# Last attention: the causal mask of the scores with keys on partitions, as a bf16 identity product that begins their accumulation

## The chip, the cores and the metric

One Trainium2 chip, one core. The metric is the device time of one execution in microseconds (us). The kernel before took 2001.97 us, the median of three runs (2001.23 to 2002.74).

## The reference

A batch of 32 sequences of 128 tokens with 128 features goes through four gated blocks: an attention over a context (16 heads), a mixture of 64 small experts, a second attention over the context, and a block with a causal self-attention and 8 experts. The change touches the last block's self-attention alone. Cut to it:

```
h = _rmsnorm(x, g1)
c = h @ w_down                                   # 64 latent features
q = _rope(split(c @ wq), pos); k = _rope(split(c @ wk), pos); v = split(c @ wv)   # 16 heads of 4
scores = jnp.einsum('bhqd,bhkd->bhqk', q, k) / jnp.sqrt(jnp.float32(HD))
scores = jnp.where(causal, scores, -jnp.inf)
attn = jax.nn.softmax(scores, axis=-1)
o = jnp.einsum('bhqk,bhkd->bhqd', attn, v)
x = x + o @ w_up
```

## The kernel before

The program is written engine by engine with semaphores, in blocks that follow each other with a barrier between them. `attend_both_ways` (line 370) is called twice: for the first attention (names `a_att_...`, 120 keys, with limits on the scores, so `clamp` is true) and for the last one (names `dt_...`, 128 keys, `clamp` false, 1446 to 1674 us of the span). Only the second call is changed.

The function takes the 32 batches through a software pipeline of rounds t = 0 to 36. The 16 heads of a batch are four groups of four; a group's scores are one product of 512 columns that uses 32 rows of the array, and the groups use different rows. The scores are made twice. With queries on partitions they go into banks 0 and 1 (line 532), and VectorE takes the row maxima from there (`row_max`, line 658). With keys on partitions ("turned", line 538) they go into banks 2 to 5, one bank for each group, where the row maxima are subtracted by one more accumulating product (`shift`, line 546), ScalarE takes the exponential of two banks at a time (line 607), and the result is, without a transposition, the stationary operand of the product with the values (line 599). Scores are in two parts (high and low) in a reduced fp32 format, so each group needs three products.

In round t TensorE's own order is: phase one (`score_phase` with groups 0, 1 of batch t and turned groups 2, 3 of batch t-2), shift A of turned groups 0, 1 of batch t-2, the transpositions of lines 567 and 573, phase two (groups 2, 3 of batch t and turned groups 0, 1 of batch t-1), shift B of turned groups 2, 3 of batch t-2, lines 589 and 592, and the 32 small products of line 599. Ahead of phase one it waits for the first phase's buffers: the keys (`s_kd`), the second row maximum of batch t-1 (`s_max`) and exponential B (`s_expB`). Ahead of phase two it waits for this round's first row maximum (`s_max`), the queries (`s_qd`) and exponential A (`s_expA`).

The causal mask is a table of 0 and -1e30. For the scores with queries on partitions it is put in by TensorE: the two products of line 526, the identity in bf16 times the mask in bf16 (`causal16`), begin the accumulation in banks 0 and 1. For the turned scores VectorE adds the transposed mask in place, two banks of 512 columns at a time: `in_place`, line 667, called behind each row maximum; `s_inB` and `s_inA` count it, and TensorE waits for them ahead of shift B and shift A. In the first attention the same place holds the limits (line 665) instead of a mask.

The setup block at the program's start loads the tables; there GpSimd makes `ident16` and `causal16` (lines 210 and 211).

## Time and profile before

| what | value |
|---|---|
| median of three runs | 2001.97 us |
| the profiled execution's own time | 2003.22 us |
| its span, first to last instruction | 2001.4 us |
| granted clock of TensorE, mean over the span | 0.928 of full speed |
| TensorE products, busy | 1762.3 us (88%) |
| VectorE, busy | 1517.2 us (76%) |
| ScalarE, busy | 1146.6 us (57%) |
| GpSimd, busy | 1166.7 us (58%) |

PE is TensorE (PEld its weight loads, which overlap the products), DVE is VectorE, ACT ScalarE, POOL GpSimd, SP SyncE. The span is what lies between the first and the last instruction of the profiled execution; its own time is 1.8 us more, and 1.25 us above the median of the runs. Busy shares are means over stages with different limits, so a stage has to be read by itself. A timeline row gives start, busy time, engine, line and operation; "x2" behind it means that two instructions are merged, and the brackets give the idle time before it and what ended that.

### The profile page before, as it was taken

Reading aid. Unit: us, or ns where it says so; the run is one execution under the profiler, and the core shown is the slowest. Engines: PE = TensorE matmul, PEld = TensorE weight load, DVE = VectorE, ACT = ScalarE, POOL = GpSimd, SP = SyncE. Lnnn points to the kernel's source line nnn. Section 1 sums busy time; section 2 is a strip of 40 time slices with the busy share of each in tenths; the row PEclk is TensorE's granted clock in tenths of the full one; section 3 lists DMA queues with packets and bytes.
Section 4 is the critical chain, followed back from the end, with each engine's and each line's share of the span. In section 5 each row is a group of like instructions: output and inputs, shape, how many; then the busy total and the mean of one; then the engine's idle time right before and its main releaser. Section 6 shows DMA issues by size and latency. Waiting matters only on the chain. (4 is left out here: it accounts for less than half of the span.)

```text
span 2001.4 us, 37718 instructions
## 1 busy us (share of the span) xinstructions
PE 1762.3 (88%) x11570; PEld 1339.4 (67%) x11570; DVE 1517.2 (76%) x3061; ACT 1146.6 (57%) x2941; POOL 1166.7 (58%) x1158
## 2 busy tenths in 40 slices
PE   3688877799999999994899999996789997799998
PEld 2355555588888888872677777775535555588886
DVE  5699978677887787767666766675769997677876
ACT  1366645555555555552677777775436666455554
POOL 4777736567776777655233333323768884667764
PEclk9699977799999999995999999998869997799999
DMA  5111100555556566430000000000000000222222
GB/s 126 47 45 46 48 17 14 129 137 136 146 143 144 129 145 146 128 83 8 5 5 5 5 5 5 1 1 1 0 1 1 0 1 17 72 79 64 82 66 69
DMA packets 99645, 115.22 MB, mean 58 GB/s; under 512 B 18064, under 2 KB 55120, under 8 KB 99504
## 3 DMA queue, kind: packets, MB, share of 16 engines
q1 hardware_dynamic: 96576, 112.14, 21.7%
q10 hardware_dynamic: 2928, 1.39, 0.3%
q8 instruction: 66, 1.08, 0.2%
q14 instruction: 75, 0.61, 0.1%
HBM read 101.82 MB, written 3.28 MB: 53 GB/s over the span
## 5 line engine op out<-in xcount | busy, mean ns | idle before, releaser
L76 POOL TENSOR_TENSOR b_moe_hid_low<-b_moe_hid,b_moe_hid_high 128x512 fp32r<-128x512 f32 x256 | 331.3, 1294 | 173.2 <-ACT b_moe_hid_high L1038 171.5
L1044 ACT ACTIVATE bank<-bank 128x512 f32<-128x512 f32 x384 | 223.5, 582 | 339.8 <-PE bank L83 339.8
L1744 POOL TENSOR_TENSOR XC<-XC,c_recip 128x480 f32<-128x480 f32 x128 | 126.8, 991 | 292.6 <-DVE c_recip L1911 292.6
L1069 DVE TENSOR_TENSOR b_moe_gu<-bank,XC 128x512 f32<-128x512 f32 x256 | 176.6, 690 | 115.7 <-PE bank L83 100.0
L76 POOL TENSOR_TENSOR e_moe_hid_low<-e_moe_hid,e_moe_hid_high 128x512 fp32r<-128x512 f32 x128 | 165.6, 1294 | 84.2 <-ACT e_moe_hid_high L1038 83.4
L1865 ACT ACTIVATE XC<-bank,c_shift 128x120 f32<-128x120 f32 x512 | 176.9, 364 | 21.2 <-DVE c_shift L1901 21.2
L71 DVE CAST c_ts_high<-bank 128x480 fp32r<-128x480 f32 x128 | 84.2, 658 | 135.0 <-PE bank L83 134.3
L1074 DVE TENSOR_TENSOR b_moe_hid<-bank,b_moe_gu 128x512 f32<-128x512 f32 x256 | 176.9, 691 | 9.3 <-POOL b_moe_hid_low L76 0.7
L1038 ACT ACTIVATE b_moe_hid_high<-b_moe_hid 128x512 fp32r<-128x512 f32 x256 | 160.0, 625 | 12.4 <-DVE b_moe_hid L1074 11.6
L1860 ACT ACTIVATE c_probT<-bank 120x512 f32<-120x512 f32 x128 | 76.6, 598 | 105.1 <-PE bank L1790 103.2
L1069 DVE TENSOR_TENSOR e_moe_gu<-bank,XC 128x512 f32<-128x512 f32 x128 | 88.4, 690 | 62.2 <-PE bank L83 51.0
L1865 ACT ACTIVATION_READ_ACCUMULATOR XC<-bank,c_shift 128x1 f32 x512 | 108.7, 212 | 0.0
L607 ACT ACTIVATE dt_probT<-bank 128x1024 f32<-128x1024 f32 x64 | 65.5, 1024 | 69.9 <-PE bank L546 69.9
L81 PE MATMUL bank<-b_moe_hid_high,b_moe_wd_high 128*128 128x512 f32 x256 | 100.0, 391 | 1.6 <-POOL b_moe_hid_low L76 1.6
L658 DVE TENSOR_REDUCE dt_negmax<-bank 128x8 f32<-128x1024 f32 x64 | 78.4, 1224 | 30.0 <-PE bank L532 13.4
L81 PE MATMUL bank<-XT_high,b_moe_wg_high 128*128 128x512 f32 (+1 forms) x256 | 100.2, 391 | 0.9 <-PEq L1181 0.9
L81 PE MATMUL bank<-XT_high,b_moe_wu_high 128*128 128x512 f32 (+1 forms) x256 | 100.2, 392 | 0.8 <-DVE b_moe_gu L1069 0.8
L83 PE MATMUL bank<-XT_low,b_moe_wg_high 128*128 128x512 f32 (+1 forms) x256 | 100.1, 391 | 0.0
L82 PE MATMUL bank<-XT_high,b_moe_wg_low 128*128 128x512 f32 (+1 forms) x256 | 100.1, 391 | 0.0
L83 PE MATMUL bank<-XT_low,b_moe_wu_high 128*128 128x512 f32 (+1 forms) x256 | 99.9, 390 | 0.0
L82 PE MATMUL bank<-XT_high,b_moe_wu_low 128*128 128x512 f32 (+1 forms) x256 | 99.9, 390 | 0.0
L83 PE MATMUL bank<-b_moe_hid_low,b_moe_wd_high 128*128 128x512 f32 x256 | 99.6, 389 | 0.0
(386 smaller groups left out, 5622.9 us busy)
## 6 DMA issues: line engine op xcount, KB each, us to landing
XC<-b_comb SPq DMA_DIRECT2D x256, 256.0 KB, 4.4
XC<-e_comb SPq DMA_DIRECT2D x64, 256.0 KB, 3.1
X<-in_x SPq DMA_DIRECT2D x4, 512.0 KB, 9.0
a_att_qs_high<-XC SPq DMA_DIRECT2D x32, 64.0 KB, 1.8
a_att_qs_low<-a_Q_low SPq DMA_DIRECT2D x32, 64.0 KB, 1.9
a_att_ks_high<-a_K_high SPq DMA_DIRECT2D x32, 64.0 KB, 1.9
a_att_ks_low<-a_K_low SPq DMA_DIRECT2D x32, 64.0 KB, 1.9
b_moe_w_gate<-in_b_wgT SPq DMA_DIRECT2D x8, 256.0 KB, 3.0
```

What stands on the lines that cost most here:

```text
L71: return eng.tensor_copy(high.bitcast(F32R), x)
L76: return eng.tensor_tensor(low.bitcast(F32R), x, high, ALU.subtract)
L81: pe.matmul(out, w[0].bitcast(F32R), x[0].bitcast(F32R), start=start, stop=False)
L82: pe.matmul(out, w[1].bitcast(F32R), x[0].bitcast(F32R), start=False, stop=False)
L83: return pe.matmul(out, w[0].bitcast(F32R), x[1].bitcast(F32R), start=False, stop=stop)
L658: return dve.tensor_reduce(negmax[u][:].rearrange("p (b r h) -> p b r h", b=2, r=2)[:, half], banks[:, 0:2, 0:HG * nk].rearrange("p b (h k ...
L1038: act.activation(hid_high[k % 4][:].bitcast(F32R), hid[k % 2][:], ACT.Copy).then_inc(s_hh, 1)
L1044: act.activation(gate_b[j % 4][:], gate_b[j % 4][:], ACT.Silu).then_inc(s_silu, 1)
L1069: dve.tensor_tensor(gu[j % 2][:], up_b[j % 2][:], comb[j // 2][:, (j % 2) // share, :], ALU.mult).then_inc(s_gu, 1)
L1074: dve.tensor_tensor(hid[j % 2][:], gate_b[j % 4][:], gu[j % 2][:], ALU.mult).then_inc(s_p, 1)
L1744: pool.tensor_tensor(prob[r % 8], prob[r % 8], recip[:, r % 8, :].unsqueeze(2).broadcast_to([P, HG, NKV]), ALU.mult).then_inc(s_norm, 1)
L1865: e = act.activation(prob[n % 8][:, h, :], score_b[n % 2][:, h * NKV:(h + 1) * NKV], ACT.Exp, bias=shift[:, n % 8, h:h + 1], accum_out=sum ...
```

## The change

A second bf16 mask, `causalT16`, is made by GpSimd at the end of the setup block: the transposed mask four times side by side, 128x512. In the last attention `score_phase` now issues, behind the two products of line 526 and ahead of the scores, one identity product per turned group (two in each phase, line 532 of the changed kernel) that begins the accumulation in that group's bank; the first turned score product accumulates onto it instead of starting. VectorE's in-place addition is gone there, with the counts `s_inA` and `s_inB` and TensorE's two waits for them. The first attention keeps its in-place limits and its waits. The values in the table are the same, 0 and -1e30 rounded to bf16.

```diff
@@ -141,6 +141,7 @@
         causal = sb("causal", [P, P])
         causalT = sb("causalT", [P, P])
         causal16 = sb("causal16", [P, HG, P], BF16)
+        causalT16 = sb("causalT16", [P, HG, P], BF16)
         ident16 = sb("ident16", [P, P], BF16)
 
         prep = ExitStack()
@@ -209,6 +210,7 @@
                 pool.wait_ge(s_load, all_loads)
                 pool.tensor_copy(ident16[:], ident[:])
                 pool.tensor_copy(causal16[:], causal[:].unsqueeze(1).broadcast_to([P, HG, P]))
+                pool.tensor_copy(causalT16[:], causalT[:].unsqueeze(1).broadcast_to([P, HG, P]))
 
             @staticmethod
             def vector(dve):
@@ -525,6 +527,10 @@
                             for g in groups:
                                 pe.matmul(bank[g % 2][:], ident16[:], causal16[:].rearrange("p h k -> p (h k)"),
                                           start=True, stop=False)
+                        if not clamp and has(bt):
+                            for g in turned:
+                                pe.matmul(turned_b[g][:], ident16[:], causalT16[:].rearrange("p h q -> p (h q)"),
+                                          start=True, stop=False)
                         for qp, kp in ((0, 0), (0, 1), (1, 0)):
                             if has(t):
                                 for g in groups:
@@ -537,7 +543,7 @@
                                     rows = group_rows(g)
                                     i = pe.matmul(turned_b[g][:], ks[vt][kp][rows, :].bitcast(F32R),
                                                   qd[vt % 2][qp][rows].rearrange("p h q -> p (h q)").bitcast(F32R),
-                                                  start=(qp + kp == 0), stop=(qp == 1))
+                                                  start=(clamp and qp + kp == 0), stop=(qp == 1))
                         return i
 
                     def shift(u, groups):
@@ -558,7 +564,8 @@
                         if has(t) or has(t - 2):
                             score_phase(t, v, (0, 1), t - 2, (v - 2) % 4, (2, 3)).then_inc(s_first, 1)
                         if has(t - 2):
-                            pe.wait_ge(s_inA, t - 1)
+                            if clamp:
+                                pe.wait_ge(s_inA, t - 1)
                             pe.wait_ge(s_mrow, t - 1)
                             shift(u, (0, 1)).then_inc(s_shA, 1)
                         if has(t - 4):
@@ -579,7 +586,8 @@
                         if has(t) or has(t - 1):
                             score_phase(t, v, (2, 3), t - 1, (v - 1) % 4, (0, 1)).then_inc(s_second, 1)
                         if has(t - 2):
-                            pe.wait_ge(s_inB, t - 1)
+                            if clamp:
+                                pe.wait_ge(s_inB, t - 1)
                             shift(u, (2, 3)).then_inc(s_shB, 1)
                         if has(t - 1):
                             pe.wait_ge(s_mrow, t)
@@ -661,17 +669,14 @@
 
                     def in_place(half):
                         both = banks[0:nk, 2 + 2 * half:4 + 2 * half, :]
-                        if clamp:
-                            return dve.tensor_scalar(both, both, limit[0:nk, 0:1], limit[0:nk, 1:2], ALU.min, ALU.max)
-                        both = both.rearrange("p b (h q) -> p (b h) q", h=HG)
-                        return dve.tensor_tensor(both, both, causalT[:].unsqueeze(1).broadcast_to([P, 2 * HG, P]), ALU.add)
+                        return dve.tensor_scalar(both, both, limit[0:nk, 0:1], limit[0:nk, 1:2], ALU.min, ALU.max)
 
                     def body(t, v):
                         u = v % 2
                         if has(t):
                             dve.wait_ge(s_first, t + 1)
                             row_max(t, u, 0).then_inc(s_max, 1)
-                        if has(t - 2):
+                        if clamp and has(t - 2):
                             dve.wait_ge(s_first, t + 1)
                             in_place(1).then_inc(s_inB, 1)
                         if has(t - 4):
@@ -685,7 +690,7 @@
                         if has(t):
                             dve.wait_ge(s_second, t + 1)
                             row_max(t, u, 1).then_inc(s_max, 1)
-                        if has(t - 1):
+                        if clamp and has(t - 1):
                             dve.wait_ge(s_second, t + 1)
                             in_place(0).then_inc(s_inA, 1)
                         if has(t):
```

One phase two of a steady round on TensorE, from its mask products to the product of line 589, before (`ident` and `causal` stand for the bf16 copies; line numbers are those of each kernel):

```order
L526 MATMUL bank<-causal,ident 128x512 x2
L532 MATMUL bank<-dt_kd_high,dt_qs_high 128x512 x2
L538 MATMUL bank<-dt_qd_high,dt_ks_high 128x512 x2
L532 MATMUL bank<-dt_kd_low,dt_qs_high 128x512 x2
L538 MATMUL bank<-dt_qd_high,dt_ks_low 128x512 x2
L532 MATMUL bank<-dt_kd_high,dt_qs_low 128x512 x2
L538 MATMUL bank<-dt_qd_low,dt_ks_high 128x512 x2
L546 MATMUL bank<-dt_mrow,dt_ones_r 128x512 x2
L589 MATMUL bank<-w_d_up,dt_headT 128x128
```

and the same place of the changed kernel:

```order
L528 MATMUL bank<-causal,ident 128x512 x2
L532 MATMUL bank<-causalT,ident 128x512 x2
L538 MATMUL bank<-dt_kd_high,dt_qs_high 128x512 x2
L544 MATMUL bank<-dt_qd_high,dt_ks_high 128x512 x2
L538 MATMUL bank<-dt_kd_low,dt_qs_high 128x512 x2
L544 MATMUL bank<-dt_qd_high,dt_ks_low 128x512 x2
L538 MATMUL bank<-dt_kd_high,dt_qs_low 128x512 x2
L544 MATMUL bank<-dt_qd_low,dt_ks_high 128x512 x2
L552 MATMUL bank<-dt_mrow,dt_ones_r 128x512 x2
L597 MATMUL bank<-w_d_up,dt_headT 128x128
```

Two products of 128x512 are new, between the mask products that were there and the scores; the rest stands in the same order. It is so in both phases of every round in which there are turned scores.

On VectorE a round of the last attention, before:

```order
L658 TENSOR_REDUCE dt_negmax<-bank 128x8
L667 TENSOR_TENSOR bank<-bank,causalT 128x1024
L680 RECIPROCAL dt_recip<-bank 128x16
L683 TENSOR_TENSOR dt_heads<-bank,dt_recip 128x128
L658 TENSOR_REDUCE dt_negmax<-bank 128x8
L667 TENSOR_TENSOR bank<-bank,causalT 128x1024
L71 CAST dt_mz<-dt_negmax 128x4x4
L76 TENSOR_TENSOR dt_mz<-dt_negmax,dt_mz 128x4x4
L709 TENSOR_TENSOR XC<-bank,XC 128x128
```

and of the changed kernel:

```order
L666 TENSOR_REDUCE dt_negmax<-bank 128x8
L685 RECIPROCAL dt_recip<-bank 128x16
L688 TENSOR_TENSOR dt_heads<-bank,dt_recip 128x128
L666 TENSOR_REDUCE dt_negmax<-bank 128x8
L71 CAST dt_mz<-dt_negmax 128x4x4
L76 TENSOR_TENSOR dt_mz<-dt_negmax,dt_mz 128x4x4
L714 TENSOR_TENSOR XC<-bank,XC 128x128
```

The two in-place additions are gone and nothing takes their place.

## Rows read from the trace of the kernel before

**Rows 1.** The page, busy time of each engine over the whole span
```profile
PE 1762.3 (88%) x11570; PEld 1339.4 (67%) x11570; DVE 1517.2 (76%) x3061; ACT 1146.6 (57%) x2941; POOL 1166.7 (58%) x1158
```

**Rows 2.** Groups by line, 1450 to 1690 us (busy, mean ns; idle before, releasers)
```profile
L658 DVE TENSOR_REDUCE dt_negmax<-bank 128x8 f32<-128x1024 f32 x64 | 78.4, 1224 | 30.0 <-PE bank L532 13.4 <-PE bank L538 11.7
L667 DVE TENSOR_TENSOR bank<-bank,causalT 128x1024 f32<-128x1024 f32 x64 | 78.2, 1222 | 1.5 <-PE bank L538 1.5
...
L526 PE MATMUL bank<-causal,ident 128*128 128x512 bf16 x128 | 42.0, 412 | 29.5 <-ACT dt_probT L607 17.7 <-POOL dt_kd_low L489 6.7 <-DVE dt_negmax L658 5.1
```

**Rows 3.** Windows (length; busy of PE, PEld, DVE, ACT, POOL; PEclk): steady stretch, one round
```profile
1540.00:1570.00 30.00, 27.33 (x343) 15.93 (x340) 28.58 (x45) 20.29 (x49) 25.44 (x35) 1.00 0.00 0
1560.05:1566.28 6.23, 5.63 (x74) 3.31 (x72) 5.87 (x10) 4.21 (x10) 5.15 (x8) 1.00 0.00 0
```

**Rows 4.** Timeline of one round (start us, us, engine line op; idle before <-releaser)
```profile
1560.05 1.22 DVE L658 TENSOR_REDUCE dt_negmax<-bank 128x8 f32<-128x1024 f32 x1
...
1560.35 1.02 ACT L607 ACTIVATE dt_probT<-bank 128x1024 f32<-128x1024 f32 x1 [1.13 <-PE bank L546]
...
1561.19 1.22 DVE L667 TENSOR_TENSOR bank<-bank,causalT 128x1024 f32<-128x1024 f32 x1
...
1561.52 0.59 PE L526 MATMUL bank<-causal,ident 128*128 128x512 bf16 x2 [0.60 <-ACT dt_probT L607]
...
1562.62 0.39 PE L538 MATMUL bank<-dt_qd_low,dt_ks_high 32*128 32x512 f32 x1
...
1562.84 0.41 PE L546 MATMUL bank<-dt_mrow,dt_ones_r 32*128 32x512 f32 x2
1563.07 1.22 DVE L658 TENSOR_REDUCE dt_negmax<-bank 128x8 f32<-128x1024 f32 x1
...
1563.70 1.08 PE L599 MATMUL bank<-dt_probT,dt_vh 128*32 128x128 f32 x32
...
1564.21 1.22 DVE L667 TENSOR_TENSOR bank<-bank,causalT 128x1024 f32<-128x1024 f32 x1
...
1564.71 0.61 PE L526 MATMUL bank<-causal,ident 128*128 128x512 bf16 x2
...
1565.82 0.40 PE L538 MATMUL bank<-dt_qd_low,dt_ks_high 32*128 32x512 f32 x2
...
1566.06 0.40 PE L546 MATMUL bank<-dt_mrow,dt_ones_r 32*128 32x512 f32 x2
1566.28 1.23 DVE L658 TENSOR_REDUCE dt_negmax<-bank 128x8 f32<-128x1024 f32 x1
```

**Rows 5.** Line 546 over the whole kernel: what it waited for, us and times
```profile
  DVE bank L665: 31.4, 72
  DVE bank L667: 2.0, 3
```

**Rows 6.** Timeline of two phases in the stage's start, at the low clock
```profile
1467.06 1.01 PE L526 MATMUL bank<-causal,ident 128*128 128x512 bf16 x2 [1.43 <-DVE dt_negmax L658]
...
1471.29 1.01 PE L526 MATMUL bank<-causal,ident 128*128 128x512 bf16 x2 [0.81 <-ACT dt_probT L607]
```

**Rows 7.** Windows, columns as before, around the rise of the granted clock
```profile
1475.00:1480.00 5.00, 3.67 (x18) 1.62 (x19) 3.55 (x6) 2.19 (x7) 4.07 (x6) 0.50 0.00 0
1480.00:1485.00 5.00, 5.00 (x50) 2.69 (x48) 3.10 (x5) 2.36 (x7) 1.76 (x4) 0.50 0.00 0
1485.00:1490.00 5.00, 4.49 (x48) 2.44 (x50) 3.63 (x6) 2.75 (x7) 4.43 (x6) 0.97 0.02 3
```

**Rows 8.** Timeline near the stage's end
```profile
1664.28 0.50 PE L546 MATMUL bank<-dt_mrow,dt_ones_r 32*128 32x512 f32 x2 [0.74 <-DVE bank L667]
```

**Rows 9.** Timeline of the end of the setup block
```profile
34.70 0.61 POOL L211 CAST causal<-causal 128x512 bf16<-128x512 f32 x1
35.78 0.59 ACT L190 ACTIVATE mT<-bank 96x512 f32<-96x512 f32 x1 [1.11 <-PE bank L199]
```

**Rows 10.** Window, columns as before, of back-to-back 512-column products in the expert stage
```profile
1730.00:1750.00 20.00, 20.00 (x90) 16.48 (x89) 16.03 (x24) 11.65 (x21) 14.89 (x13) 1.00 0.30 97
```

## The prediction

> **What bounds the kernel now.** I read the page first: TensorE is busy for 88% of the span, VectorE for 76% [rows 1]. That is a mean over stages, so next the groups of the last attention, which alone is changed. There VectorE's two costliest groups are the row maxima and the mask additions that the change removes, 78.4 and 78.2 us busy [rows 2]. The windows then say how full the engines are: in 30 us of the steady part VectorE is busy 28.58 us, TensorE 27.33, and in one round of 6.23 us they are at 5.87 and 5.63 [rows 3]. By these shares alone VectorE is the fuller engine and its relief is welcome. Which of the two sets the pace is read from the timeline and from who ends whose waits.
>
> In the timeline of a round [rows 4] TensorE has one gap, 0.60 us ahead of phase two's mask products at 1561.52. It is put down to exponential A, which ended at 1560.35 + 1.02 = 1561.37; the first row maximum, for which the same products wait, ended at 1560.05 + 1.22 = 1561.27. From 1561.52 to the end of the next phase one TensorE runs without a wait, through scores, shift B, the products with the values (1563.70) and the mask products of phase one (1564.71). The group rows say the same of the whole stage: of the waits ahead of line 526, 17.7 us are for the exponential [rows 2].
>
> So the question is what starts those two. The second row maximum starts at 1563.07, while the last score product of its phase ends at 1562.62 + 0.39 = 1563.01; the next one starts at 1566.28, its scores end at 1565.82 + 0.40 = 1566.22 [rows 4]. Each begins 0.06 us behind TensorE, though VectorE is busy nearly all the time: it is ready just in time and is not what TensorE waits for. Nor do the additions hold the shifts: the addition that starts at 1561.19 ends at 1562.41 and its shift starts at 1562.84, the one from 1564.21 ends at 1565.43 and its shift starts at 1566.06 [rows 4]. Over the whole stage shifts waited 2.0 us for the mask additions, against 31.4 us for the limits of the first attention in the same place of the code [rows 5]. **The bound of the stage is the loop TensorE, exponential A, TensorE**, with VectorE close behind.
>
> **The change part by part.**
> - *Additions removed.* 64 x 1.222 us [rows 2] leave VectorE, 2.44 us of each round. On the path they stand only in the stage's last rounds: shift B waited 0.74 us for one at 1664.28 [rows 8]. I count a gain of 0.74 us. Late next would be nothing new: the row maximum still starts at the scores' end, and exponential A still behind shift A.
> - *Products added.* Two per phase, so four per batch and 128 in all. None can go into the gap: they stand in the queue behind the waits for row maximum and exponential, and behind the old mask products. In phase one they push the end of the scores, and with it the row maximum and shift A, in phase two everything behind. All 128 lie on the loop. A pair of such products takes 0.61 us from first start to last end (0.59 in phase two), and a single 512-column product shows 0.39 [rows 4], so the second adds 0.20 to 0.22 us. In the expert stage 90 products, nearly all of this width, fill 20.00 us, 0.222 each [rows 10]. I take 0.215.
> - *Their price by the clock.* At the stage's start the granted clock is 0.50, which is the 1.2 GHz level, and at 1485 it is back at 2.4 GHz [rows 7]. Phases there are 1471.29 - 1467.06 = 4.23 us apart [rows 6], and five of those with turned scores begin before 1484: the two shown, one ahead of them and two behind. Ten products at twice 0.215: 4.3 us. The other 118 x 0.215 = 25.4 us.
> - *One copy more in setup.* GpSimd's cast of the other mask took 0.61 us and ended at 34.70 + 0.61 = 35.31; a second such ends at 35.92, and ScalarE's last copy of that block ends at 35.78 + 0.59 = 36.37 [rows 9]. Hidden; uncovered it would cost 0.6 us at most.
> - *Two waits removed on TensorE, none added.* No queue is passed, no DMA moves.
>
> The sum is 4.3 + 25.4 - 0.7 = **29.0 us slower**, of which 27 rounds or so in the steady part give 0.86 us each: a round of 6.23 becomes 7.09. The profiled execution at 2003.22 would become 2032.2; against the median of the runs, 1.25 lower, it is 2001.97 + 29.0 = 2031.0. With 0.20 and 0.222 for a product, and with none or all of the tail's 0.74 gained, the sum goes from 26.9 to 30.6: 2028.9 to 2032.6.
>
> The Trainium skill (page "TensorE: Matmul & The Clock Gate", section "Back-to-back issue gap") gives some 131 ns for each 512-column product in a sustained stream of loads and products. By that the 128 would cost 16.8 us as an estimate, and the kernel come to some 2018. The rows here don't bear it out, with 0.20 to 0.222 us [rows 4, 10].
>
> **The rivals.**
> - *The clock rises earlier in the stage's start.* It rose between 1480 and 1485 only once TensorE was busy without a pause, 5.00 of 5.00 us; in the 5 us before it had 3.67 and stayed at 0.50 [rows 7]. The new products make the busy stretches of these phases 0.86 us longer and leave the gaps as they are, so a rise one to four phases sooner is possible. A phase at the low clock would take 4.23 + 0.86 = 5.09 us, at the full clock half a round plus the pair, 3.11 + 0.43 = 3.5, so 1.5 us is saved for each: 2025 to 2029.5, I say 2026.5. Against it: a gap of about 0.8 us stays in each phase [rows 6]. The same page of the Trainium skill, in "Part 1: The HAM clock gate (the "warmup" mystery)", says that the slow state is the default and sustained activity releases it, which is this rival; the rise in rows 7 agrees with it.
> - *VectorE sets the pace after all, and its relief pays back a part.* For it: 28.58 of 30 us [rows 3]. Then TensorE's gap of 0.60 a round would shrink, by up to 0.55 x 27 = 15 us: 2016 to 2028. Against it: the 0.06 us above, and the exponential as the later of the two waits.
> - *The other side: faster.* VectorE sets the pace and the products also cost little, because they stream in with the others. The round would then be TensorE's busy time plus four products, 5.63 + 4p, and it decides at p = (6.23 - 5.63) / 4 = 0.15 us. With p = 0.10 a round is 6.03, 27 rounds save 5.4 us: 1996.6. Against it stand both the 0.20 to 0.22 us of every such pair and the order of the waits.
> - *The accumulation costs more.* A score product of 32 rows now adds to what a product of the full array wrote just before, four groups wait for four such products, and no row shows that for the turned banks. At 0.15 us more in each of 64 phases: 2040.6.
> - *The change does nothing to the time*, because the products hide in time that I don't see: 2002.
>
> **How the numbers follow.** Chances: the forecast 0.68, the clock rising early 0.14, VectorE's relief paying part back 0.06, faster 0.03, costlier accumulation 0.07, nothing 0.02. The likeliest gives 2031. The range takes in the forecast's bounds and most of the early clock, and reaches some way to the costlier case: 2024 to 2035 leaves out nearly all of the last four, about 0.17. A measurement of this kernel can tell about 0.2% (4 us) from no change. Slower by more than that: 0.68 + 0.14 + 0.07 and the relief's 0.06 are 0.95; within it 0.02; faster 0.03.
>
> **What the profile after would show.** Right: the steady round is 7.05 to 7.12 us; line 532 of the changed kernel has 128 bf16 products; the gap ahead of phase two's mask products is still about 0.6 us and still ended by the exponential; row maxima still start 0.06 us after the scores; VectorE is busy about 5.87 - 2.44 = 3.4 us of a round, half of it; the stage is 29 us longer and all others are unchanged. The early clock would show as windows at 1.00 within the first three rounds. The relief theory would show as the gap shrinking under 0.3 us, the costlier accumulation as score products that start over 0.4 us behind the last mask product's start. A round under 6.9 us, or a setup block that ends later, would make the prediction wrong.

## The result, and the profile after

The changed kernel takes 2026.57 us, the median of four runs (2025.37 to 2027.71), where the kernel before took 2001.6 beside it: 1.0128 times as long, with a 95% interval of 1.0115 to 1.0140. That is 25 us slower. The forecast was 29 us slower, 2031, in a range from 2024 to 2035; the measured time lies inside it, but below the 2028.9 to 2032.6 that the forecast's own terms allowed.

The groups of the last attention in the changed kernel (busy us, mean ns; idle time before and its releasers), against [rows 2]:

```profile
L666 DVE TENSOR_REDUCE dt_negmax<-bank 128x8 f32<-128x1024 f32 x64 | 78.4, 1224 | 118.7 <-PE bank L544 105.3 <-PE bank L538 13.4
...
L528 PE MATMUL bank<-causal,ident 128*128 128x512 bf16 x128 | 40.4, 398 | 30.0 <-ACT dt_probT L615 18.1 <-POOL dt_kd_low L491 6.7 <-DVE dt_negmax L666 5.1
L532 PE MATMUL bank<-causalT,ident 128*128 128x512 bf16 x128 | 39.0, 387 | 0.6 <-ACT dt_probT L615 0.6
```

VectorE's additions are gone, and its idle time ahead of the row maxima went from 30.0 to 118.7 us. The 128 new products are there, and next to nothing is waited for ahead of them. The waits ahead of the old mask products are what they were: 30.0 us against 29.5, the exponential first.

The windows of the steady part and of one round (us; busy of PE, PEld, DVE, ACT, POOL; granted clock), against [rows 3]:

```profile
1540.00:1570.00 30.00, 27.87 (x330) 15.79 (x322) 14.53 (x30) 17.67 (x43) 21.98 (x31) 1.00 0.00 0
1561.14:1568.13 6.99, 6.47 (x80) 3.68 (x77) 3.54 (x7) 4.21 (x11) 5.13 (x7) 1.00 0.00 0
```

VectorE fell from 28.58 to 14.53 of 30 us. TensorE is the fuller engine now. One round of the timeline, against [rows 4]:

```profile
1561.14 0.60 PE L528 MATMUL bank<-causal,ident 128*128 128x512 bf16 x2
...
1561.58 0.59 PE L532 MATMUL bank<-causalT,ident 128*128 128x512 bf16 x2
...
1562.68 0.40 PE L544 MATMUL bank<-dt_qd_low,dt_ks_high 32*128 32x512 f32 x2
...
1563.12 1.23 DVE L666 TENSOR_REDUCE dt_negmax<-bank 128x8 f32<-128x1024 f32 x1 [1.69 <-PE bank L544]
...
1563.34 1.02 ACT L615 ACTIVATE dt_probT<-bank 128x1024 f32<-128x1024 f32 x1 [1.47 <-PE bank L552]
...
1564.51 0.59 PE L528 MATMUL bank<-causal,ident 128*128 128x512 bf16 x2 [0.52 <-ACT dt_probT L615]
...
1564.94 0.59 PE L532 MATMUL bank<-causalT,ident 128*128 128x512 bf16 x2
...
1566.04 0.39 PE L544 MATMUL bank<-dt_qd_low,dt_ks_high 32*128 32x512 f32 x1
...
1566.48 1.23 DVE L666 TENSOR_REDUCE dt_negmax<-bank 128x8 f32<-128x1024 f32 x1 [1.65 <-PE bank L544]
...
1568.13 0.60 PE L528 MATMUL bank<-causal,ident 128*128 128x512 bf16 x2
```

From the mask products of one phase one to those of the next it is 6.99 us. The pair of line 532 starts 0.43 us behind the pair of line 528, in both phases. The gap ahead of phase two is 0.52 us and still ended by exponential A. Row maxima start where the scores end: the score product at 1562.68 ends at 1563.08, the maximum starts at 1563.12.

Single rounds differ by some 0.1 us, so the mean over 27 of them is the better number. It runs from line 526's (now 528's) products in phase two of round 4 to those of round 31. Before:

```profile
1487.84 0.59 PE L526 MATMUL bank<-causal,ident 128*128 128x512 bf16 x2 [0.51 <-ACT dt_probT L607]
```
```profile
1653.84 0.59 PE L526 MATMUL bank<-causal,ident 128*128 128x512 bf16 x2 [0.52 <-ACT dt_probT L607]
```

After:

```profile
1487.67 0.59 PE L528 MATMUL bank<-causal,ident 128*128 128x512 bf16 x2 [0.51 <-ACT dt_probT L615]
```
```profile
1676.71 0.59 PE L528 MATMUL bank<-causal,ident 128*128 128x512 bf16 x2 [0.52 <-ACT dt_probT L615]
```

(1653.84 - 1487.84) / 27 = 6.148 us before, (1676.71 - 1487.67) / 27 = 7.001 after: 0.853 a round, 23.0 us in all. The prediction had 0.86 for the step; its 6.23 for the round before was read from one round, 0.08 above this mean.

The stage's start is where it went otherwise. Windows of the changed kernel, against [rows 7]:

```profile
1465.00:1470.00 5.00, 3.58 (x18) 1.28 (x16) 2.04 (x2) 0.05 (x1) 2.98 (x5) 0.50 0.00 0
1470.00:1475.00 5.00, 4.05 (x22) 1.78 (x20) 1.51 (x3) 2.04 (x5) 2.28 (x4) 0.75 0.00 0
```

and the starts of the mask products there, against [rows 6]:

```profile
1464.40 1.03 PE L528 MATMUL bank<-causal,ident 128*128 128x512 bf16 x2 [0.92 <-DVE dt_negmax L666]
...
1469.30 1.01 PE L528 MATMUL bank<-causal,ident 128*128 128x512 bf16 x2 [1.43 <-DVE dt_negmax L666]
...
1474.13 0.59 PE L528 MATMUL bank<-causal,ident 128*128 128x512 bf16 x2 [0.95 <-ACT dt_probT L615]
...
1477.60 0.59 PE L528 MATMUL bank<-causal,ident 128*128 128x512 bf16 x2 [1.31 <-ACT dt_probT L615]
```

At the low clock a phase takes 4.90 us, but the clock is up 10 to 15 us sooner, counted from the program's start ([rows 7] have it at 0.50 up to 1485), and the third and fourth phase shown are only 3.47 us apart. From the stage's first product to phase two of round 4 it is 35.12 us after and 36.67 before: 1.6 us less, where the forecast's sum had 4.7 more (five pairs at the low clock and one at the high).

At the end shift B no longer waits, against [rows 8]:

```profile
1688.05 0.50 PE L552 MATMUL bank<-dt_mrow,dt_ones_r 32*128 32x512 f32 x2
```

and the cast in the setup block is hidden, as its end at 35.92 lies ahead of ScalarE's at 36.47, against [rows 9]:

```profile
35.31 0.61 POOL L213 CAST causalT<-causalT 128x512 bf16<-128x512 f32 x1
35.88 0.59 ACT L191 ACTIVATE mT<-bank 96x512 f32<-96x512 f32 x1 [1.11 <-PE bank L200]
```

### The profile page after: what moved, and what is told of

It is laid out like the page before. It is cut to its first block and busy times, and to the rows that moved or that the text cites. A ratio compares the mean times of both kernels' runs of the same rounds, so it can differ in the third digit from the quotient of the medians.

```text
span 2025.9 us, 37879 instructions
## 1 busy us (share of the span) xinstructions
PE 1789.8 (88%) x11698; PEld 1353.1 (67%) x11698; DVE 1444.5 (71%) x2997; ACT 1146.7 (57%) x2941; POOL 1167.6 (58%) x1159
## 5 line engine op out<-in xcount | busy, mean ns | idle before, releaser
L666 DVE TENSOR_REDUCE dt_negmax<-bank 128x8 f32<-128x1024 f32 x64 | 78.4, 1224 | 118.7 <-PE bank L544 105.3
L82 PE MATMUL bank<-b_moe_hid_high,b_moe_wd_low 128*128 128x512 f32 x256 | 99.7, 389 | 0.0
```

Of the source, the lines that this page charges most:

```text
L82: pe.matmul(out, w[1].bitcast(F32R), x[0].bitcast(F32R), start=False, stop=False)
L666: return dve.tensor_reduce(negmax[u][:].rearrange("p (b r h) -> p b r h", b=2, r=2)[:, half], banks[:, 0:2, 0:HG * nk].rearrange("p b (h k ...
```

## The experiments

The kernels and their stages, worked out from each one's timeline in the way shown above: *start* is from the stage's first mask product to phase two of round 4, *round* the mean of 27, *end* from phase two of round 31 to the first load of the stage behind it (issued once the attention is through), *stage* their sum. The last column but one is the 5 us window in which the granted clock leaves 0.50 for good, counted from the program's start, with the stage's first product. The last is how far behind that product the rise comes, worked out from the window's mean clock with 0.50 ahead of the rise and 1.00 behind it. In nine of the traces (no_mask to split_before, and half_late_split) the record of the stage's first product is missing and the timeline starts with the second, 0.38 us later. There the first product is taken from its weight load, which starts 0.03 us ahead of it in the kernels that have both.

| kernel | median us | ratio to before (95%) | start | round | end | stage | clock rises (first product) | us behind it |
|---|---|---|---|---|---|---|---|---|
| before | 2001.6 to 2004.7 | 1 | 36.67 | 6.148 | 20.41 | 223.1 | 1485-1490 (1451.2) | 34 |
| after | 2026.6 | 1.0128 (1.0115-1.0140) | 35.12 | 7.001 | 21.11 | 245.3 | 1470-1475 (1452.6) | 20 |
| no_mask | 2000.7 | 0.9992 (0.9983-1.0001) | 36.58 | 6.148 | 19.14 | 221.7 | 1480-1485 (1448.1) | 34 |
| both | 2024.8 | 1.0105 (1.0090-1.0120) | 35.25 | 7.000 | 21.87 | 246.1 | 1465-1470 (1449.7) | 20 |
| fill_only | 1999.8 | 0.9984 (0.9975-0.9993) | 34.59 | 6.152 | 20.20 | 220.9 | 1465-1470 (1448.2) | 20 |
| rest_only | 2027.0 | 1.0118 (1.0103-1.0134) | 37.03 | 6.994 | 21.89 | 247.8 | 1485-1490 (1451.6) | 34 |
| double | 2054.0 | 1.0256 (1.0240-1.0271) | 36.60 | 7.869 | 22.83 | 271.9 | 1470-1475 (1454.2) | 16 |
| late | 2011.8 | 1.0041 (1.0029-1.0054) | 34.68 | 6.577 | 20.73 | 233.0 | 1470-1475 (1449.8) | 23 |
| half_late | 1997.6 | 0.9974 (0.9960-0.9987) | 31.94 | 6.146 | 19.78 | 217.6 | 1470-1475 (1451.0) | 20 |
| split_before | 1999.2 | 0.9979 (0.9968-0.9989) | 35.91 | 6.039 | 20.47 | 219.4 | 1490-1495 (1457.8) | 33 |
| warm_before | 1995.4 | 0.9968 (0.9955-0.9981) | 30.23 | 6.152 | 20.18 | 216.5 | 1460-1465 (1449.9) | 13.5 |
| half_late_split | 1994.6 | 0.9961 (0.9949-0.9974) | 31.59 | 6.040 | 19.86 | 214.5 | 1465-1470 (1449.9) | 20 |
| warm_split_y | 1989.4 | 0.9929 (0.9916-0.9942) | 29.97 | 5.864 | 21.20 | 209.5 | 1460-1465 (1451.0) | 13.5 |
| warm_after | 2023.8 | 1.0098 (1.0081-1.0115) | 32.92 | 6.999 | 21.15 | 243.0 | 1465-1470 (1452.3) | 13.5 |

The kernel before was run beside each set: its medians were 2002.6 for no_mask to rest_only, 2002.7 for double to split_before, 2002.1 for warm_before to warm_split_y and 2004.7 for warm_after. Its single runs lie between 1998.6 and 2006.6, and the stage's first product comes between 1448.1 and 1457.8 in kernels that are the same up to there but for a cast and the fillers of the last set. So a microsecond or two of a difference between whole runs says little, and the stage column is the better measure.

Three accounts of the 25 us stood against each other. *Price*: every product costs 0.215 us on the loop and the additions cost nothing but the tail. *Relief*: VectorE's additions did cost something, and their removal paid back 4 us. *Clock*: the products brought the rise of the clock forward in the stage's start.

**no_mask.** The additions removed alone.

```diff
-                pool.tensor_copy(causal16[:], causal[:].unsqueeze(1).broadcast_to([P, HG, P]))
+                pool.memset(causal16[:], 0.0)
...
-                        if has(t - 2):
+                        if clamp and has(t - 2):
                             dve.wait_ge(s_first, t + 1)
                             in_place(1).then_inc(s_inB, 1)
```

(and so for `in_place(0)` and for TensorE's two waits)

> The kernel before with VectorE's 64 mask additions taken out of the last attention together with TensorE's two waits for them, and nothing in their place; the mask of line 526 is all zeros so that the values stay finite. It leaves out the whole causal mask of the last attention. If VectorE's additions are not on the loop (my account), only the stage's tail gains: 0.7 to 2 us less than the kernel before, so 1999.6 to 2001. If VectorE's relief is what made the measured 25 us less than my 29, this kernel must show it alone: 4 us or more less than the kernel before, at most 1997.6.

It measured 2000.72 against 2002.62, 1.9 us less, with an interval that includes no change. Windows around the clock's rise and of the steady part:

```profile
1480.00:1485.00 5.00, 4.16 (x54) 2.50 (x47) 2.58 (x6) 3.25 (x8) 3.67 (x5) 0.80 0.02 3
1540.00:1570.00 30.00, 27.06 (x355) 16.44 (x358) 16.98 (x34) 20.29 (x49) 24.92 (x36) 1.00 0.00 0
```

VectorE is busy 16.98 us of 30 instead of 28.58, and the round stays at 6.148 us to the third decimal. In the steady part the additions cost nothing. At the end 1.3 us went.

**both.** The changed kernel with the additions and their waits put back; the diff is that of no_mask the other way round, on the changed kernel.

> The changed kernel with VectorE's additions and TensorE's waits for them back in place, so that the turned scores are masked twice (-2e30 instead of -1e30, the same result after the exponential). If the additions are hidden, it takes the changed kernel's time plus the tail's 0.7: 2026.6 to 2028. If their removal paid back some 4 us, it takes 2030 or more.

2024.76 us: below the 2026.6 to 2028 expected and no slower than the changed kernel. The round is 7.000 against 7.001. The stage is 0.9 us longer and begins 2.9 us earlier. At the stage's end it is 0.76 us longer, which is the tail's term of 0.74. Relief is out, from both sides. Against the kernel before that ran beside it, this kernel is 22.1 us slower, near the 23 us of its stage.

**fill_only** and **rest_only.** The new products in the first rounds only, and from round 4 on only (`not fill(t)` in the line below); the additions stay in both.

```diff
+                    def fill(t):
+                        return isinstance(t, int) and t < 4
...
+                        if not clamp and has(bt) and fill(t):
+                            for g in turned:
+                                pe.matmul(turned_b[g][:], ident16[:], causalT16[:].rearrange("p h q -> p (h q)"),
+                                          start=True, stop=False)
```

> The kernel before, with the new products added in the rounds 0 to 3 only (five phases, ten products, the mask twice there). By the sum as forecast, with the clock rising as late as before, it takes 4.3 us more than the kernel before: 2005.9. If the new products bring the rise of the clock forward, by the changed kernel's trace (36.70 us before, 35.1 after, from the stage's first product to round 4's second phase) it takes 1 to 3 us less: 1998.6 to 2000.6, and the granted clock is at its high level from 1470 to 1475 instead of 1485.

> The kernel before, with the new products added from round 4 on only (59 pairs, 118 products, the mask twice there). My account: 118 x 0.215 = 25.4 us more than the kernel before, 2027, the clock rising at about 1485 as before. If a product costs less than 0.215 on the loop, for instance because the gap ahead of phase two shrinks, it is under 2023.

fill_only is 2.8 us *faster* than the kernel before (1999.81 against 2002.62), with ten products more; 2.2 us of that lie in the stage. Its windows:

```profile
1465.00:1470.00 5.00, 3.83 (x20) 1.79 (x21) 2.90 (x5) 1.51 (x4) 2.39 (x3) 0.71 0.00 0
1470.00:1475.00 5.00, 3.68 (x35) 1.82 (x33) 3.41 (x5) 1.97 (x6) 2.16 (x5) 1.00 0.00 0
```

and those of rest_only, which has the same work as the kernel before in rounds 0 to 3:

```profile
1480.00:1485.00 5.00, 4.81 (x48) 2.70 (x49) 3.14 (x3) 2.50 (x8) 1.76 (x4) 0.50 0.00 0
1485.00:1490.00 5.00, 4.16 (x38) 2.27 (x39) 3.31 (x7) 2.66 (x6) 4.88 (x7) 0.94 0.01 3
```

In fill_only the clock leaves 0.50 between 1465 and 1470, in rest_only at 1485. rest_only measured 2027.03, 24.4 us more than before, with 118 products. So one change does two things: its 118 later products cost some 25 us, its first ten bring a little.

**double.** Each new product twice.

```diff
-                            for g in turned:
+                            for r, g in [(r, g) for r in range(2) for g in turned]:
                                 pe.matmul(turned_b[g][:], ident16[:], causalT16[:].rearrange("p h q -> p (h q)"),
-                                          start=True, stop=False)
+                                          start=(r == 0), stop=False)
```

> The changed kernel with each new product issued twice (the mask twice on the turned scores), so 128 more of them. If each of the new products costs its 0.215 us on the loop, this takes 25 to 28 us more than the changed kernel: 2051 to 2055. If part of them lie in waits, the step is under 20 us.

2053.98 us, 27.4 more than the changed kernel's 2026.57. The round grew by 0.868 us for four products, 0.217 each. In its timeline the four of a phase and the first score product behind them:

```profile
1561.95 1.03 PE L532 MATMUL bank<-causalT,ident 128*128 128x512 bf16 x4
...
1562.90 0.49 PE L538 MATMUL bank<-dt_kd_high,dt_qs_high 32*128 32x512 f32 x2
```

The price is the same for the second set as for the first, so no part of them lies in a wait. At the stage's start the clock comes up sooner again, 16 us behind the first product against 20.

**late.** The products of turned groups 2 and 3 moved into the gap.

```diff
                             pe.transpose(side_b[:, 0:P], mz[1 - u][:], ident[:]).then_inc(s_mt, 1)
+                        if not clamp and has(t - 2):
+                            for g in (2, 3):
+                                pe.matmul(turned_b[g][:], ident16[:], causalT16[:].rearrange("p h q -> p (h q)"),
+                                          start=False, stop=False, skip_group_check=True)
```

(in `score_phase` the products stay for groups 0 and 1 only, and the scores of 2 and 3 start their banks as before)

> The changed kernel with the two products of turned groups 2 and 3 moved from the start of phase one to behind the transposition of line 573, just ahead of the waits of phase two, where TensorE has its gap of 0.5 to 0.6 us. Same work, other place. If it is the place in the loop that costs, 0.43 us of each of some 30 rounds goes: 11 to 13 us less than the changed kernel, 2013.5 to 2016. If it is TensorE's total work that costs, it takes the same time as the changed kernel.

2011.77 us, 14.8 less than the changed kernel, more than the 11 to 13 expected; the profiled stage is 12.3 us shorter and begins 2.8 us earlier. The round is 6.577, shorter by 0.424, which is the pair's 0.43. The gap in its timeline:

```profile
1562.45 0.27 PE L580 MATMUL bank<-ident,dt_mz 128*128 128x128 f32 x1
...
1562.56 0.59 PE L583 MATMUL bank<-causalT,ident 128*128 128x512 bf16 x2
...
1563.31 0.59 PE L528 MATMUL bank<-causal,ident 128*128 128x512 bf16 x2 [0.15 <-ACT dt_probT L619]
```

The moved pair starts at 1562.56 behind the transposition, and of the gap 0.15 us is left. Same instructions, same number, 11.4 us less in 27 rounds (12.3 in the stage): it is the place that costs.

**half_late.** Groups 2 and 3 as in late, groups 0 and 1 by VectorE as before. The diff is against late.

```diff
-                        if clamp and has(t - 1):
+                        if has(t - 1):
                             dve.wait_ge(s_second, t + 1)
                             in_place(0).then_inc(s_inA, 1)
```

(`in_place` adds the mask again, TensorE's wait for `s_inA` is back, and the products of `score_phase` are gone)

> Only half of the change: turned groups 2 and 3 get their mask by products in the gap ahead of phase two, turned groups 0 and 1 by VectorE's addition as before. By the loop account nothing is added on the loop and nothing that was on it is taken away: the kernel before to within 2 us, or 1 to 3 us less where the products fill the pauses at the stage's start and the clock rises earlier: 1999 to 2003. If TensorE's total work counts, 12 us more than before.

1997.64 against 2002.67, 5.0 us less than before, more than expected. The round is 6.146, as before: the pair in the gap is free.

```profile
1466.92 1.01 PE L528 MATMUL bank<-causal,ident 128*128 128x512 bf16 x2 [1.43 <-DVE dt_negmax L665]
...
1471.14 0.59 PE L528 MATMUL bank<-causal,ident 128*128 128x512 bf16 x2
...
1562.06 0.59 PE L578 MATMUL bank<-causalT,ident 128*128 128x512 bf16 x2
...
1562.74 0.59 PE L528 MATMUL bank<-causal,ident 128*128 128x512 bf16 x2
```

What it gains it gains in the stage's start, 31.94 against 36.67 us, and 0.6 at the end. The clock comes up 20 us behind the first product, as in the changed kernel, and there too the pair in the gap costs nothing: the phase from 1466.92 to 1471.14, at the low clock, takes 4.22 us with it and took 4.23 before. VectorE has half of its additions less here, which by no_mask is worth nothing in a round.

**split_before.** The kernel before with one wait moved.

```diff
-                        if has(t - 1):
-                            pe.wait_ge(s_qd, t)
-                            wait(pe, s_expA, t - 1)
+                        def turned_ready():
+                            if has(t - 1):
+                                pe.wait_ge(s_qd, t)
+                                wait(pe, s_expA, t - 1)
                         if has(t) or has(t - 1):
-                            score_phase(t, v, (2, 3), t - 1, (v - 1) % 4, (0, 1)).then_inc(s_second, 1)
+                            score_phase(t, v, (2, 3), t - 1, (v - 1) % 4, (0, 1), turned_ready).then_inc(s_second, 1)
```

(`score_phase` calls it behind the products of line 526)

> The kernel before with one wait of TensorE moved: in phase two it waits for exponential A and the queries only ahead of the turned scores, behind the mask products of line 526, instead of ahead of them. These then start when the row maximum ends, some 0.1 to 0.2 us earlier in each round, while 0.43 us of mask products cover the rest of the exponential. If the loop is as I read it, 3 to 5 us less than before: 1997.5 to 1999.5.

1999.21 against 2002.67, 3.5 less; the round is 0.109 us shorter, 2.9 in 27.

```profile
1564.81 1.23 DVE L661 TENSOR_REDUCE dt_negmax<-bank 128x8 f32<-128x1024 f32 x1
...
1565.10 1.02 ACT L610 ACTIVATE dt_probT<-bank 128x1024 f32<-128x1024 f32 x1 [1.13 <-PE bank L548]
...
1566.09 0.60 PE L526 MATMUL bank<-causal,ident 128*128 128x512 bf16 x2 [0.42 <-DVE dt_negmax L661]
```

The mask products start at 1566.09, 0.05 us behind the maximum's end at 1566.04 and ahead of the exponential's end at 1566.12. The loop is read rightly: the exponential ended the wait in the kernel before, and with it out of the way the row maximum does, a tenth of a microsecond sooner.

**warm_before.** Products that nobody reads in TensorE's pauses at the stage's start.

```diff
+                    def keep_busy(n):
+                        for _ in range(n):
+                            pe.matmul(out_b[:], ident16[:], causal16[:].rearrange("p h k -> p (h k)"), start=True, stop=True)
+                    if not clamp:
+                        keep_busy(10)
                     pe.wait_ge(s_clear, 2)
...
+                        if not clamp and isinstance(t, int) and 0 < t < 4:
+                            keep_busy(3)
...
+                        if not clamp and isinstance(t, int) and t < 4:
+                            keep_busy(3)
                         if has(t):
                             pe.wait_ge(s_max, 2 * t + 1)
```

> The kernel before with products that nobody reads (identity times mask into bank 6) in TensorE's pauses at the stage's start: ten ahead of the first round and three ahead of each phase's waits in rounds 0 to 3. The mask stays with VectorE as before. If what matters for the clock is that TensorE has no pause there, and not the new products as such, the high level comes before 1460 and all phases of the start take some 3 us instead of 4.2: 5 to 9 us less than before, 1993.5 to 1997.5. If the filling costs more than it gives, or the clock rises no earlier than with the mask products (18 to 19 us behind the stage's first product), 1999 or more.

1995.35 against 2002.13, 6.8 us less, though the clock came up between 1460 and 1465, not before 1460. Its timeline around the rise (line 522 are the fillers):

```profile
1460.65 1.49 PE L522 MATMUL bank<-causal,ident 128*128 128x512 bf16 x3
...
1461.93 1.06 PE L531 MATMUL bank<-causal,ident 128*128 128x512 bf16 x2
...
1464.24 0.59 PE L522 MATMUL bank<-causal,ident 128*128 128x512 bf16 x2 [0.16 <-issue]
...
1465.51 0.59 PE L531 MATMUL bank<-causal,ident 128*128 128x512 bf16 x2 [0.68 <-DVE dt_negmax L667]
```

Up to 1461.93 TensorE has no pause between fillers and mask products; from 1464.24 on the products show 0.59 us for a pair, which is the high clock. The start is 30.23 us, 6.4 less than before. The mask stays with VectorE here, so products that have nothing to do with the change bring the rise forward too. Whether the filled pause or the added work does it is not shown: fill_only leaves the pauses open and has the rise at 20 us instead of 34, and late, with half of its new products in the gap, has it at 23.

**half_late_split.** The two edits together.

> half_late (mask of turned groups 2 and 3 by products in the gap, of 0 and 1 by VectorE) together with the moved wait of split_before. The gap is nearly full in half_late, the products of line 528 start 0.68 us behind the late mask products and could start after 0.43 to 0.5: up to 0.2 us of a round. 2 to 5 us less than half_late's 1997.6: 1993 to 1996.

1994.56 against 2002.13; the round is 6.040, no shorter than with the moved wait alone (6.039), and 0.106 shorter than in half_late. The time is 3.1 us less than half_late's, inside what was expected, while the 0.2 us of a round was an upper bound of which half came.

**warm_split_y.** warm_before, split_before, and the projection of line 589 ahead of the transposition of line 573.

```diff
+                        if not clamp and has(t - 5):
+                            pe.wait_ge(s_headT, t - 4)
+                            wait(pe, s_out, t - 5)
+                            pe.matmul(side_b[:, P:P + D], headT[1 - u][:], wo[:], start=True, stop=True).then_inc(s_y, 1)
                         if has(t - 1):
                             pe.wait_ge(s_mz, mz_steps * t)
...
-                        if has(t - 5):
+                        if clamp and has(t - 5):
```

> The kernel before with three edits: the filled pauses of warm_before, the moved wait of split_before, and the projection of line 589 moved from behind shift B into the gap ahead of phase two's waits (ahead of the transposition of line 573). The projection takes about 0.2 us out of the loop in each of 27 rounds, up to 5 us, if the gap of 0.4 us that split_before leaves takes it up. With 5 to 9 us for the filling and 3.5 for the wait: 1986 to 1992.

1989.37 against 2002.13, 12.8 us less: the fastest of all, and faster than both kernels of the case. The round is 5.864, 0.175 less than with the moved wait alone. Its gap, and its steady window:

```profile
1562.51 0.39 PE L581 MATMUL bank<-w_d_up,dt_headT 128*128 128x128 f32 x2
...
1562.73 0.27 PE L586 MATMUL bank<-ident,dt_mz 128*128 128x128 f32 x1
...
1563.24 0.60 PE L531 MATMUL bank<-causal,ident 128*128 128x512 bf16 x2 [0.23 <-DVE dt_negmax L674]
```
```profile
1540.00:1570.00 30.00, 27.86 (x365) 16.81 (x372) 29.54 (x46) 21.25 (x53) 26.34 (x37) 1.00 0.00 0
```

The gap is down to 0.23 us, and VectorE is busy 29.54 of 30 us: hardly any of its time is left. Here, and not in the kernel before, its relief may pay. That was not tried.

**warm_after.** The changed kernel with the same fillers as warm_before.

> The changed kernel with the filled pauses of warm_before. Both then pass the stage's start at the high clock, so that the difference to warm_before's 1995.4 us is the products' price without the clock: 128 x 0.215 less the tail's 0.74 is 26.8 us, 2022.2. If removing VectorE's additions pays anything back beyond the tail, it is under 2019; if my price was too low, over 2025.

2023.79 us where the kernel before had 2004.69 beside it, 19.1 more; warm_before was 6.8 less than its own. The step between the two is 25.9 us by that, 26.5 by the stages (243.0 - 216.5), against 26.8 expected. With the clock's part nearly equal on both sides the price of the sum holds.

## Why the prediction was right, and where it was off

- **What bounds the stage: right.** The loop of TensorE and exponential A was read from a gap of 0.60 us and starts 0.06 us behind TensorE. no_mask (6.148 us a round, as before) and both (7.000, as after) show that VectorE's additions were not part of it although the engine was busy for 95% of the time, and split_before and late that the gap is where I took it to be.
- **The products' price: right.** 0.853 us a round against 0.86, and 0.868 in double. The 131 ns of the Trainium skill ("TensorE: Matmul & The Clock Gate", "Back-to-back issue gap") would have made it 0.52; the runs show 0.213 (after) and 0.217 (double) for each. That leaves nothing for a costlier accumulation, which the rival put at 0.15 us in each phase.
- **The tail: right in size.** 0.74 us was forecast, both has it at 0.76 against the changed kernel.
- **The setup's copy: hidden,** as forecast.
- **The clock at the stage's start: wrong.** The step that failed is "Ten products at twice 0.215: 4.3 us", which took the clock's rise to stay where it was. A pair at the low clock did cost what I said (1469.30 - 1464.40 = 4.90 us for the phase that took 4.04 before), but the clock rose some 20 us behind the stage's first product instead of 33 to 34 (the windows in the table), and the start came out 1.6 us shorter than before instead of 4.7 longer. That is 6.3 us, and it is the rival that I gave 0.14, with 2026.5 as its time. Its argument was there, and the rows for it; I weighed it down because a pause of 0.8 us stayed in each phase. The prediction also put the rise before between 1480 and 1485; [rows 7] show 0.50 up to 1485 and 0.97 behind it, so it came right behind 1485. In every kernel here that adds products to these rounds the rise came earlier, and in none that doesn't. The Trainium skill (page "TensorE: Matmul & The Clock Gate", section "Part 1: The HAM clock gate (the "warmup" mystery)") says that activity releases the slow state. The direction agrees, with the rise at 20 us (after) against 34 (before); that it comes while the pauses stay is not explained by it.
- **The time: inside the range, outside the forecast's own terms.** 2026.57 us lies in the range only because that was drawn to take in the early clock. That it comes within 0.1 us of that rival's 2026.5 is luck in part: the stage by itself gives 2001.97 + 22.2 = 2024.2, and 2.3 us of the profiled spans' difference come from outside it.
- **The profile after: in part.** The mean round is 7.00 us where 7.05 to 7.12 was said, the gap 0.52 (0.6 was said; it was 0.51 to 0.52 before too, in the rows of rounds 4 and 31), and the stage 22.2 us longer where 29 was said. VectorE at 3.54 us of a round, the exponential as what ends the gap, and the windows at 1.00 from 1475 on, named there as the sign of the early clock, came.
- **How it adds up.** The stage is 245.3 - 223.1 = 22.2 us longer: -1.6 in the start, 23.0 in the rounds, 0.7 at the end. The forecast of 29.0 less the start's 6.3 is 22.7. The median shows 25, and the profiled spans 24.5: 1.4 us of that lies ahead of the stage's first product (1452.55 against 1451.17), 0.9 behind the stage. As code that is the same up to there but for a cast reaches that point between 1448.1 and 1457.8, I take these for the spread between executions and not for an effect of the change. The granted clock far ahead of the change goes with it. Between 900 and 1000 us it is 0.72 before, 0.66 after, and 0.62 in split_before, which reaches the stage last:

```profile
900.00:1000.00 100.00, 65.91 (x333) 48.78 (x333) 67.85 (x192) 44.88 (x156) 42.96 (x37) 0.72 0.03 6
900.00:1000.00 100.00, 66.94 (x316) 49.62 (x317) 65.89 (x189) 43.63 (x151) 42.47 (x36) 0.66 0.03 6
900.00:1000.00 100.00, 64.77 (x283) 47.94 (x284) 63.45 (x183) 40.17 (x135) 40.59 (x35) 0.62 0.02 6
```

No run here makes that clock differ by an edit, so it stays a reading of the traces.

What stays open is why a stretch lengthened by 0.86 us is enough when the pauses remain. The runs show that it is, and that the 31 products in the pauses bring the rise to 13.5 us. They do not show whether pauses or added work decide, nor where the border lies.

## What to carry to other kernels

An engine that is busy 95% of the time can still be off the loop. Look at how soon its instructions start behind their releaser, and whether anybody waits for their ends, before work is moved away from it to the engine that is on the loop. The same two products cost 0.43 us a round at the head of a phase and nothing in the gap ahead of the next wait: where a product may go at any point of an accumulation, it goes into the pause. And a stage that begins at the low clock is a place of its own in the sum, since work added there changes when the clock rises; filling TensorE's pauses with idle products gave 6.8 us for a few lines.

## What the runs showed of the hardware

- Ten more products at the start of a stage made the whole kernel 2.8 us faster (fill_only), and 31 products that nobody reads 6.8 us (warm_before). With pauses of 0.8 to 1.4 us in each phase of about 4 us the granted clock stayed at 0.50 for 33 to 34 us from the stage's first product (before, no_mask, rest_only, split_before); with busy stretches 0.86 us longer for some 20 (after, both, fill_only), with twice that for 16 (double), and with the pauses filled for 13.5 (warm_before, warm_split_y, warm_after).
- A 512-column bf16 product whose stationary operand is the same as that of the product before it costs 0.213 us of TensorE's time as the third and fourth in a row (after) and 0.217 as the fifth and sixth (double), with its own weight load hidden.
- To begin an accumulation with a product over the full array and go on with products of 32 rows, or to put it in the middle, ahead of the last one (late), cost no time beyond the product's own (a round 0.853 us longer for four products in after, 0.429 for the two that late leaves at the head of a phase, nothing for the two in the gap).
